# Expert rows of a mixture-of-experts stage: three batches by indirect DMA instead of two

## What is computed

```python
capacity = int(512 * 2.0 / 8) + 1                       # 129 tokens per expert and batch
scores = softmax(einsum('bsd,ed->bse', x, router_w))    # 8 experts
gate_vals, sel_idx = top_k(swapaxes(scores, 1, 2), capacity)
tokens = x[b_idx, sel_idx]                              # gather, 4 batches x 8 experts x 129 rows
h = gelu(einsum('becd,edh->bech', tokens, w1) + b1)     # 128 -> 512
y = einsum('bech,ehd->becd', h, w2) + b2                # 512 -> 128
out = zeros_like(x).at[b_idx, sel_idx].add(y * gate_vals[..., None])
```

## Time and profile before

| | us |
|---|---|
| median of 3 runs | 755.59 (753.18 to 757.89) |
| the profiled execution, time | 753.51 |
| its span, first to last instruction | 751.6 |
| TensorE matmuls busy | 634.6 (84%) |
| VectorE busy | 584.4 (78%) |
| ScalarE busy | 497.2 (66%) |
| GpSimd busy | 457.1 (61%) |

### The profile page before, as it was taken

The page is one execution under the profiler, slowest core; times in us unless marked ns, Lnnn a source line. Parts: engine busy times, 40 slices in busy tenths (PEclk is TensorE's granted clock), DMA queues, the critical chain, the costliest instruction groups (busy, mean ns, idle before and its releaser), DMA issues. The chain is left out here.

```text
span 751.6 us, 8865 instructions
## 1 busy us (share of the span) xinstructions
PE 634.6 (84%) x2909; PEld 394.8 (53%) x2909; DVE 584.4 (78%) x820; ACT 497.2 (66%) x935; POOL 457.1 (61%) x259
## 2 busy tenths in 40 slices
PE   3955777688699999999988699999999972599992
PEld 2443455433455555555422455565655561499982
DVE  6794897557799999999765799999999958734521
ACT  3643534468999898989568999898989553033320
POOL 0136664100598989889600498989888615358866
PEclk9866788698799999999998699999999975599997
DMA  5000000001132323333001223232332181023323
GB/s 200 0 3 1 1 1 0 1 2 61 53 88 98 99 90 93 98 90 105 31 3 44 58 86 99 97 99 84 100 99 90 52 308 57 3 27 41 40 30 28
DMA packets 30780, 48.05 MB, mean 64 GB/s; under 512 B 3736, under 2 KB 12328, under 8 KB 30224
## 3 DMA queue, kind: packets, MB, share of 16 engines
q1 hardware_dynamic: 25600, 44.45, 18.4%
q0 software_dynamic: 5136, 3.05, 3.7%
HBM read 42.98 MB, written 4.49 MB: 63 GB/s over the span
## 5 line engine op out<-in xcount | busy, mean ns | idle before, releaser
L481 POOL TENSOR_TENSOR hc_all<-hs_all,c_row 128x1024 f32<-128x1024 f32 x87 | 205.0, 2369 | 122.0 <-DVE hs_all L1674 121.2
L1149 PE MATMUL ps<-hc_all,ident 128*128 128x512 f32 x508 | 237.1, 598 | 2.7 <-POOL hc_all L481 2.7
L1674 DVE TENSOR_TENSOR_SCAN hs_all<-da,ps 128x1024 f32<-128x1024 f32 x88 | 197.9, 2270 | 14.1 <-ACT da L811 9.1
L811 ACT ACTIVATE da<-big,a_neg 128x511 f32<-128x511 f32 x256 | 169.3, 709 | 30.7 <-DVE w_ffn L1674 29.1
L1149 PEld LDWEIGHTS ps<-hc_all,ident 128*128 128x128 f32 x508 | 90.2, 192 | 86.9 <-issue 77.0
L481 POOL TENSOR_TENSOR hc_all<-w_ffn,c_row 128x1024 f32<-128x1024 f32 x40 | 94.7, 2368 | 29.7 <-DVE w_ffn L1674 26.5
L1674 DVE TENSOR_TENSOR_SCAN w_ffn<-da,ps 128x1024 f32<-128x1024 f32 x40 | 91.4, 2285 | 3.8 <-ACT da L811 0.9
L1169 PE MATMUL ps<-ident,dbu 128*128 128x128 f32 x464 | 62.2, 279 | 11.2 <-ACT dbu L786 6.0
L1169 PEld LDWEIGHTS ps<-ident,dbu 128*128 128x128 f32 x464 | 54.2, 143 | 25.8 <-issue 18.7
L547 POOL DMA_INDIRECT out<-hc_all,hs_all x32 | 52.2, 1632 | 11.9 <-issue 8.8
L888 ACT ACTIVATE big<-ps,b 128x516 f32<-128x516 f32 x32 | 22.1, 690 | 47.3 <-PE ps L1340 47.3
(11 more groups left out here) (309 smaller groups left out, 1025.5 us busy)
## 6 DMA issues: line engine op xcount, KB each, us to landing
c_row<-c_rows SPq DMA_DIRECT2D x128, 256.0 KB, 3.1
tmpA<-w_in SPq DMA_DIRECT2D x2, 1024.0 KB, 7.2
tmpB<-w_in SPq DMA_DIRECT2D x2, 1024.0 KB, 9.3
x_tok<-x_in SPq DMA_DIRECT2D x2, 512.0 KB, 5.7
out<-x_tok SPq DMA_DIRECT2D x1, 1024.0 KB, 11.9
xm_rows<-xn SPq DMA_DIRECT2D x1, 1024.0 KB, 5.0
w_mod<-w_mod_in SPq DMA_DIRECT2D x2, 384.0 KB, 6.5
w_ffn<-w_ffn_in SPq DMA_DIRECT2D x1, 560.0 KB, 7.7
```

The source lines that it names most:

```text
L481: nc.gpsimd.tensor_tensor(hc[:, n % 4, :, :], hs3[HS_BUF[n]].rearrange("p (i s) -> p i s", i=IC), c_row[:, n % 4, :].unsqueeze(1).to_broad ...
L811: ins = nc.scalar.activation(da[:, n % 2, i, 1:S], dtT[:, b, i, 1:S], ACT.Exp, scale=a_neg[:, l, i, n:n + 1])
L1149: mm = nc.tensor.matmul(ps[:, YS + i, :], ident[:], hc[:, n % 4, i, :], start=(n == 0), stop=(n == NS - 1))
L1674: v.tensor_tensor_scan(hs3[HS_BUF[n]], decay, pair.rearrange("p i s -> p (i s)"), 0.0, ALU.mult, ALU.add).then_inc(c_scan, 1)
```

## The change

`BY_DMA` grows from batches 2 and 3 to batches 1, 2 and 3, the buffer of fetched rows from two to three tiles for each parity, and the count that TensorE waits for from 32 to 48 per expert (an indirect DMA adds 16). Nothing else is edited.

```diff
--- before.py
+++ after.py
@@ -275,8 +275,8 @@
         gelu_last = hc_all[:, 2752:2752 + HC * B].rearrange("p (c b) -> p c b", c=HC)
         b2 = y_sb[:].rearrange("p i s -> p (i s)").rearrange("p (e d) -> p e d", e=E)
         XG, LIST, HH, YY = 0, 1, 2, 6
-        BY_DMA = [2, 3]
-        x_rows_dma = hc_all[:, 2816:2816 + 4 * D].rearrange("p (k j d) -> p k j d", k=2, j=2)
+        BY_DMA = [1, 2, 3]
+        x_rows_dma = hc_all[:, 2816:2816 + 6 * D].rearrange("p (k j d) -> p k j d", k=2, j=3)
         LG_AT, YL_AT, YLT_AT = 128, 304, 340
 
         def chunk_at(e, c):
@@ -1308,7 +1308,7 @@
                             mm = nc.tensor.matmul(ps[:, XG, b * P:(b + 1) * P], x_parts[:, k, b * TB + c, :], pick[:, e % 2, b, c, :],
                                                   start=(c == 0 and k == 0), stop=(c == TB - 1 and k == 2))
                 if e:
-                    pe.wait_ge(ld_rows[e % 2], 32 * ((e + 1) // 2 if e % 2 else e // 2))
+                    pe.wait_ge(ld_rows[e % 2], 48 * ((e + 1) // 2 if e % 2 else e // 2))
                     for j, b in enumerate(BY_DMA):
                         mm = nc.tensor.transpose(ps[:, XG, b * P:(b + 1) * P], x_rows_dma[:, e % 2, j, :], ident[:])
                 mm.then_inc(e_gather, 1)
```

## The result

| | before | changed |
|---|---|---|
| median of 13 runs, us | 754.18 | 760.79 |
| range, us | 751.08 to 757.89 | 757.82 to 768.46 |
| profiled execution, span | 751.6 | 759.4 |

The ratio is 1.0091 with a 95% interval of 1.0063 to 1.0120: slower by 0.9%, 6.6 us between the medians where the forecast was +5.9.

What follows compares the result with a forecast made beforehand. TensorE and GpSimd were both taken as full; GpSimd's extra fetches set the cost: +0.3 and +6.4, less 0.8 repaid at the end, +5.9 us, giving 761.5 us on the median, range 757.5 to 767.

Steps and rivals of the forecast that it cites:

- Two full engines: Experts' stage: TensorE and GpSimd are both full at once, with periods of 10.19 and 10.2 us a turn.
- GpSimd's sum: GpSimd's full queue, experts 3 to 7: one more fetch each at 1.28 us, +6.4 us; its turn becomes 11.5 us.
- rival 4: GpSimd: the 3.21 us scatter shrinks to 1.6, or the third fetch issues faster; +1 to +4 us, chance 0.11.
- The two early fetches: Expert 1's extra fetch is hidden in GpSimd's idle time, costing nothing; expert 2's delays the first scatter by 0.3 us.
- The end: L539 waits for expert 5's last scatter to land, starting at 735.2; 2.94 us of idle time part repaid, -0.8 us.
- TensorE's new wait: TensorE waits in `gather` for fetched rows from expert 4 on, at most 1.9 us a turn, losing its 3.9 us.
- Rival 1: TensorE's clock falls in the new waits; decides at three turns or more; about +9 us, 764.5 us, chance 0.18.
- Rival 2: VectorE's one-hots hold GpSimd's fetches 1.6 us in four or five turns; +12 to +14, 768 us, chance 0.09.
- The paragraph on the port: Whether VectorE's one-hots block GpSimd's issue through a shared SBUF port; one scatter showed no full blocking, so no term.

## Why the prediction was right, and where not

The forecast was +5.9 us, and 761.5 us on the median of three runs that it started from; +6.6 and 760.79 were measured. The account of what fills the stage was right, but the number is in part luck: the experts' stage grew by 10.1 us in the first pair of profiles, not by 5.9.

**Two full engines.** Right. Adding the fetch alone costs what the change costs (1.0087 and 1.0091); taking TensorE's work alone gains nothing (1.0019); one fetch instead of two gains nothing either (1.0003).

**GpSimd's sum.** From the scatter of 666.52 to that of 724.81 were 58.3 us; in the changed kernel, 664.50 to 732.44, 67.9 us: +9.7. Five fetches of 1.28 us are the +6.4 of the forecast. The long scatter of 3.21 us shrank to 1.73 (-1.5; rival 4, which I had at 0.11), and the holds of fetches added 5.1; the rest, -0.3, is spread over the other issues. With +0.3 ahead of the first scatter, -0.4 at L539 and +0.6 behind it, this makes the 10.1 us. The mis-sized term is the last: the step said "small holds of 0.2 us a turn are inside my forecast", and it was 1.0 us a turn in this profile. With the holds taken away from both kernels, on one chip, the third fetch costs 755.49 - 749.89 = 5.6 us, close to the +5.9 that was worked out without them. The profiles agree: from the fetch of the last tokens to the end the changed kernel takes 114.0 and 113.6 us, 10 more than the kernel before; with an operand in PSUM it takes 107.1, which is 4.8 and 5.7 more than the 102.3 and 101.4. Why the medians with the holds differ by 6.6 us only, and not by 10, is open; in the profiles the stages ahead were quicker by chance in the changed kernel.

**The two early fetches.** Right: no wait of TensorE for expert 1's or 2's rows, and three fetches of 0.94 us ahead of the first scatter.

**The end.** Right in kind: L539 is released by a landing. It starts 4.07 us after the last scatter of expert 5, and not 3.7 as the sum had it (before: 4.49), so 0.4 us was repaid and not 0.8. Behind it the eight scatters keep their pace, and the span ends 6.3 us after the start of the last one instead of 5.8.

**TensorE's new wait.** It came from expert 3 on rather than 4, 0.7 to 3.5 us instead of at most 1.9, because a held fetch lands late. Expert 7's, which the forecast had, did not come: TensorE was late itself behind the clock's fall.

**Rival 1, the clock,** came true as an event and not as a cost. It fell twice, and behind a wait of 1.61 us in the kernel with the moved one-hots too (0.83 from 700 to 710 us), where one of 1.57 us before it had left the clock full:

```profile
691.85 0.55 PE L1313 MATMUL ps<-ident,hc_all 128*128 128x128 f32 x3 [1.57 <-DMA hc_all<-xm_rows,hs_all]
692.64 3.82 PE L1373 MATMUL ps<-tmpB,big 128*128 128x128 f32 x32
...
703.30 0.55 PE L1313 MATMUL ps<-ident,hc_all 128*128 128x128 f32 x3 [1.61 <-DMA hc_all<-xm_rows,hs_all]
704.09 5.45 PE L1373 MATMUL ps<-tmpB,big 128*128 128x128 f32 x32
```

I had asked three turns or more for it to decide. GpSimd had no wait for a sum in any turn, so TensorE caught up each time.

**Rival 2, the holds,** was the half-right one, at 0.09 too low. I weighed the row that is held against those that aren't, and took the count of rows for the odds. The paragraph on the port went wrong in the same way: one scatter that was not held to the end of the one-hots does not show that no DMA is, and the fetch of the last tokens, 4.29 us under six one-hots, was in the same trace. Which DMA lies under the one-hots is what the change moves. A fetch that does is held in most cases (28 of 39), a scatter less often (8 of 26). The Trainium skill (SBUF — State Buffer, "Who interferes with whom") says that a VectorE instruction with two SBUF inputs contends with a GpSimd instruction that reads SBUF. The runs agree: with one input in PSUM all fetches take 0.94 to 1.12 us. That a hold can be absent though the fetch begins under the one-hots (11 of the 39) is not explained by it.

## What to carry to other kernels

Where the chain of waits runs on one engine, look for another that never waits: here its queue of indirect DMAs, each preceded by "issue" alone, was as full as TensorE, and work moved onto it was paid in full and gained nothing on the other engine. Look at the longest of a group of equal DMA issues and at what VectorE does in that stretch; if it is an operation on two SBUF operands, put one of them in PSUM, or the issue elsewhere in time.

## What the runs showed of the hardware

- An indirect DMA's issue of 128 rows holds GpSimd for 0.94 to 1.12 us when it fetches and 1.55 to 1.63 us when it scatters with accumulation, where it is not held, plus 0.30 us between two that follow at once.
- A fetch whose issue begins under back-to-back one-hots of 0.62 us each can be held to the end of all of them, up to 2 us (3.2 for the fetch of the last tokens, under six of them), and not only to the end of the one that runs: the full holds of fetches end 0.82 to 0.98 us after the last one-hot. Seven scatters were held fully too, and end 1.44 to 1.52 us after it; in each case nearly the whole plain issue is still to come. Others got in between (1.29 us), and the scatter of 678.32 lost only 0.2 us. What decides it is open.
- TensorE's clock fell from 2.4 to 1.2 GHz behind waits of 2.2 and 3.5 us in the changed kernel, and behind 1.61 us with the moved one-hots; in the changed kernel each fall cost 1.5 to 2.2 us on the outputs behind it. The length of the last wait alone does not tell: waits of 1.57, 1.58 and 1.66 us in other places left the clock full, and in the second profile of the changed kernel it stood at 0.50 from 732 to 734 us, where the last wait had been 0.41 us.
